# Quantised feed-forward in three stages cut another way: gate matmuls by themselves, the sigmoid in one stage with the second matmuls, 16-bit integers for the quantised values

## What is computed

```
x    = act_qdq(layernorm(h))             # scale = max|x| over the WHOLE batch / 32767, then round(x / scale) * scale
up   = act_qdq(x @ q(w_up).T)
gate = act_qdq(x @ q(w_gate).T)
sig  = clip(round(sigmoid(gate) * 65536), 0, 65535) / 65536
gate = act_qdq(gate * sig)
o    = act_qdq(gate * up)
h    = h + o @ q(w_down).T
```

## Time and profile before

| what | value |
|---|---|
| median of 3 runs | 5746.14 us |
| profiled execution, span from first to last instruction | 5746.7 us (no time of its own is recorded beside the span) |
| mean granted TensorE clock, share of full | 0.851 |
| `phase_b`, first matmul to last | 617.8 to 1058 us |
| `phase_c`, first ScalarE instruction to last of VectorE | 1071.6 to 1286.9 us |
| `phase_d`, first load issued to last of VectorE | 1291.6 to 1499.1 us |
| rest of the kernel | 0 to 617 us, and 1500 us to the end |

### The profile page before, as it was taken

How to read it: one execution, slowest core, us unless ns; L and a number is a source line. 1 busy time by engine, 2 the same in 40 slices (tenths; PEclk the granted TensorE clock), 3 DMA queues, 4 the chain that set the end, 5 groups by cost and what they waited for, 6 DMA issues and landing times. The chain is left out here.

```text
span 5746.7 us, 99792 instructions
## 1 busy us (share of the span) xinstructions
PE 4422.5 (77%) x26575; PEld 2884.0 (50%) x26575; DVE 3816.5 (66%) x9299; ACT 2478.7 (43%) x5698; POOL 596.5 (10%) x928
## 2 busy tenths in 40 slices
PE   6999788300388885878787776776999998689898
PEld 5777566200255553555555555554555554344444
DVE  4555333588687877777767764555777777477776
ACT  2222333565333333677777762222666666200000
POOL 0111000000000001000000001111111111122221
PEclk9999899655699997777777787887999999899998
DMA  2222233679644443222222225555333333211110
GB/s 81 74 75 68 105 140 139 196 240 396 229 132 124 132 124 91 62 71 71 71 71 71 71 52 144 156 156 139 85 91 92 92 90 88 63 46 47 49 47 25
DMA packets 380380, 617.00 MB, mean 107 GB/s; under 512 B 43575, under 2 KB 310389, under 8 KB 380277
## 3 DMA queue, kind: packets, MB, share of 16 engines
q1 hardware_dynamic: 367956, 614.35, 36.6%
q0 software_dynamic: 12320, 1.40, 0.2%
HBM read 345.02 MB, written 269.21 MB: 107 GB/s over the span
## 5 line engine op out<-in xcount | busy, mean ns | idle before, releaser
L1670 DVE TENSOR_REDUCE e_neg<-ps 91x1 f32<-91x273 f32 x1536 | 571.8, 427 | 139.2 <-PE ps L1491 131.8
L1603 ACT ACTIVATE e_probT<-ps 91x273 f32<-91x273 f32 x1536 | 491.6, 392 | 291.7 <-PE ps L1491 290.9
L1218 PE MATMUL ps<-k_downT,f_o 128*91 128x256 f32 x1152 | 259.7, 385 | 455.9 <-DVE f_o L1126 455.7
L2345 PE MATMUL ps<-m_we,m_xT 128*128 128x512 f32 x1104 | 530.8, 630 | 0.0
L1218 PEld LDWEIGHTS ps<-k_downT,f_o 128*91 128x91 f32 x1152 | 182.8, 161 | 524.5 <-issue 456.9
L1489 PE MATMUL ps<-c_mask_kq,c_identb 91*91 91x91 bf16 x1536 | 322.7, 241 | 105.9 <-ACT g_probT L1603 74.3
L1491 PE MATMUL ps<-e_k,e_q 96*91 96x273 bf16 x1536 | 344.3, 306 | 62.9 <-DMA e_k<-s_parts 28.1
L2279 DVE SCALAR_TENSOR_TENSOR m_acc<-ps,m_weight,m_acc 128x256 f32<-128x256 f32 x552 | 261.7, 481 | 185.7 <-PE ps L2345 175.9
L1491 PE MATMUL ps<-g_q,g_k 102*91 102x273 bf16 (+5 forms) x1536 | 328.5, 294 | 50.6 <-DVEq L1676 49.9
L2345 PEld LDWEIGHTS ps<-m_we,m_xT 128*128 128x128 f32 x1104 | 214.8, 202 | 227.9 <-issue 213.5
L1491 PE MATMUL ps<-e_q,e_k 128*91 128x273 bf16 x1536 | 285.7, 290 | 40.1 <-DMA e_q<-e_shift 38.2
(11 more groups left out here) (306 smaller groups left out, 9733.9 us busy)
## 6 DMA issues: line engine op xcount, KB each, us to landing
s_gate<-b_gu SPq DMA_DIRECT2D x32, 819.0 KB, 4.7
s_up<-b_gu SPq DMA_DIRECT2D x32, 819.0 KB, 6.1
c_g<-s_gate SPq DMA_DIRECT2D x32, 819.0 KB, 7.2
s_gated<-c_g SPq DMA_DIRECT2D x32, 819.0 KB, 8.6
d_g<-s_gated SPq DMA_DIRECT2D x32, 819.0 KB, 10.4
d_u<-s_up SPq DMA_DIRECT2D x32, 819.0 KB, 10.7
s_o<-d_o SPq DMA_DIRECT2D x32, 819.0 KB
f_o<-s_o SPq DMA_DIRECT2D x32, 819.0 KB, 4.8
```

What stands on the lines that cost most here:

```text
L1218: last = nc.tensor.matmul(ps[0:R, t // 2, (t % 2) * D:(t % 2 + 1) * D], o[:, u, k, t * R:(t + 1) * R], downT[:, k, :], start=(k == 0), sto ...
L1603: nc.scalar.activation(probT[0:R, p % 8, b, :], src, ACT.Exp, scale=float(HD) ** 0.5 if kinds[h] == COS else 1.0)\
L1670: last = nc.vector.tensor_reduce(neg[:, u, t, h:h + 1], src, AX.X, ALU.max, negate=True)
L2345: last = nc.tensor.matmul(ps[0:R, EBANK[m % 4], :], xT[:, u, k, t * R:(t + 1) * R], we[:, k, 2 * p:2 * p + 2, :].rearrange("p e d -> p (e ...
```

## The change

`phase_b` becomes `gate_stage`: only the gate matmuls; the rounded x is also stored to DRAM (`xq`). `up_stage` loads `xq` and gate, does the up matmuls, and beside them the rounding of gate, the sigmoid, the product and the maxima of gated and of up. `product_stage` takes the place of `phase_d`. All three are ordered by `pipeline`. PSUM is evacuated two banks at a time (128x546). ScalarE now writes x/scale directly into a 16-bit integer tile (the conversion rounds), so the separate VectorE rounding of gate, gated and up is gone, and the scales are folded into the scalar of one `scalar_tensor_tensor`.

```diff
+def multiply_pairs(nc, pe, ps, w, x, S, n):
+    for m in range(FP):                                   # FP = 3
+        pe.wait_ge(S["out"].sem, S["out"].at(back(n, 1), m + 1))   # back(n, 1): the image before
+        for f in (2 * m, 2 * m + 1):
+            for k in range(CT):
+                last = nc.tensor.matmul(ps[:, f, 0:T], w[:, k, f * 128:(f + 1) * 128], x[:, k, :], ...)
+        last.then_inc(S["mm"].sem, 1)
 # gate_stage, SyncE
+            def store_xq(n, u, i):
+                sp.wait_ge(S["xq"].sem, S["xq"].at(n))
+                sp.dma_start(xq_dram[batch_of(n)], x[:, u] ...)
+            def next_x(n, u, i):
+                    sp.wait_ge(S["mm"].sem, S["mm"].at(n))
+                    sp.wait_ge(xq_stored[u], 16 * (i + 1))
+                    load((n[0], n[1] + 2), u)
+            def store_gate(n, u, i):
+                sp.wait_ge(S["out"].sem, S["out"].at(n))
+            pipeline(sp, NB, ((store_xq, 1), (next_x, 0), (store_gate, 0)))
 # gate_stage, ScalarE, VectorE, TensorE
-                    for m in range(2 * FT):
-                        act.wait_ge(S["mm"].sem, S["mm"].at(n, m + 1))
-                        nc.scalar.copy(gu[:, u, m // FT, m % FT, :], ps[:, 4 * u + m % 4, 0:T])
+                for m in range(FP):
+                    act.wait_ge(S["mm"].sem, S["mm"].at(n, m + 1))
+                    nc.scalar.copy(gate[:, u, 2 * m:2 * m + 2, :], ps[:, 2 * m:2 * m + 2, 0:T])
+            pipeline(act, NB, ((divide, 1), (copy_gate, 0)))
+            pipeline(dve, NB, ((quantise, 1), (maximum, 0)))
+            pipeline(pe, NB, ((multiply, 0),))
 # up_stage
+        steps = sb("steps", [128, 2, N], mybir.dt.int16)
+        sig_steps = sb("sig_steps", [128, 2, N], mybir.dt.uint16)
+            pipeline(sp, NB, ((next_g, 1), (next_x, 0), (store_up, 0), (store_gated, 0)))
-                nc.scalar.activation(gm[:, u], g[:, u], ACT.Identity, scale=inv, bias=magic)
+                nc.scalar.activation(steps[:, u], g[:, u], ACT.Identity, scale=inv)
-                nc.scalar.activation(sg[:, u], gq[:, u], ACT.Sigmoid)
-                nc.scalar.activation(sm[:, u], sg[:, u], ACT.Identity, scale=65536.0, bias=magic)
+                nc.scalar.activation(sig[:, u], steps[:, u], ACT.Sigmoid, scale=scale)
+            pipeline(act, NB, ((divide, 1), (copy_up(0, 1), 0), (sigmoid, 1), (copy_up(1, FP), 0)))
-                nc.vector.tensor_scalar(gq[:, u], gm[:, u], MAGIC, scale, ALU.subtract, ALU.mult)
-                nc.vector.tensor_scalar(sm[:, u], sm[:, u], MAGIC + 65535.0, MAGIC, ALU.min, ALU.subtract)
+                nc.vector.tensor_scalar(sig_steps[:, u], sig[:, u], 65536.0, 65535.0, ALU.mult, ALU.min)
-                nc.vector.scalar_tensor_tensor(out=g2[:, u], in0=sm[:, u], scalar=1.0 / 65536.0,
-                                               in1=gq[:, u], op0=ALU.mult, op1=ALU.mult)
+                nc.vector.scalar_tensor_tensor(out=gated[:, u], in0=sig_steps[:, u], scalar=fine[:],
+                                               in1=steps[:, u], op0=ALU.mult, op1=ALU.mult)
+            pipeline(dve, NB, ((round_sigmoid, 0), (maximum_gated, -1), (product, 0), (maximum_up, -1)))
+            def multiply(n, u, i):
+                pe.wait_ge(x_loaded[u], 16 * (i + 1))
+                multiply_pairs(nc, pe, ps, upT, x[:, u], S, n)
 # product_stage
+            pipeline(sp, NB, ((following_loads, 1), (store, 0)))
-                        nc.scalar.activation(rounded[k][:, u], src[k][:, u], ACT.Identity, scale=inv[k],
-                                             bias=magic)
+                    nc.scalar.activation(steps[k][:, u], src[k][:, u], ACT.Identity, scale=inv[k])  # int16
-                        nc.vector.tensor_scalar(quant[k][:, u], rounded[k][:, u], MAGIC, scale[k], ...)
-                    nc.vector.tensor_tensor(o[:, u], quant["g"][:, u], quant["u"][:, u], ALU.mult)
+                nc.vector.scalar_tensor_tensor(out=o[:, u], in0=steps["g"][:, u], scalar=both[:],
+                                               in1=steps["u"][:, u], op0=ALU.mult, op1=ALU.mult)
+            pipeline(dve, NB, ((product, 0), (maximum, -1)))
```

More of the change, by code:

```diff
@@ L637, in _, with divide @@
                 S[k].give(act)
[L638 to L648, removed]
[L649 to L652 removed]
+            def divide(n, u, i):
+                act.wait_ge(x_loaded[u], 16 * (i + 1))
+                act.wait_ge(S["xq"].sem, S["xq"].at(back(n, 2)))
+                nc.scalar.activation(xm[:, u], x[:, u], ACT.Identity, scale=inv, bias=magic)\
+                    .then_inc(S["xm"].sem, 1)
@@ L654, in _, with copy_gate @@
+            def copy_gate(n, u, i):
+                act.wait_ge(stored[u], 16 * i)
+                act.wait_ge(S["max"].sem, S["max"].at(back(n, 2)))
+                for m in range(FP):
+                    act.wait_ge(S["mm"].sem, S["mm"].at(n, m + 1))
+                    nc.scalar.copy(gate[:, u, 2 * m:2 * m + 2, :], ps[:, 2 * m:2 * m + 2, 0:T])\
+                        .then_inc(S["out"].sem, 1)
+            pipeline(act, NB, ((divide, 1), (copy_gate, 0)))
         @block.vector
         def _(dve):
-            for k in ("xq", "newg", "maxg", "newu", "maxu"):
+            for k in ("xq", "new", "max"):
@@ new lines, in _, with divide, sigmoid, copy_up @@
+        @block.scalar
+        def _(act):
+            for k in ("steps", "sig", "out"):
+                S[k].give(act)
+            def divide(n, u, i):
+                act.wait_ge(g_loaded[u], 16 * (i + 1))
+                act.wait_ge(S["gated"].sem, S["gated"].at(back(n, 2)))
+                nc.scalar.activation(steps[:, u], g[:, u], ACT.Identity, scale=inv).then_inc(S["steps"].sem, 1)
+            def sigmoid(n, u, i):
+                act.wait_ge(S["steps"].sem, S["steps"].at(n))
+                act.wait_ge(S["sig_steps"].sem, S["sig_steps"].at(back(n, 2)))
+                nc.scalar.activation(sig[:, u], steps[:, u], ACT.Sigmoid, scale=scale).then_inc(S["sig"].sem, 1)
+            def copy_up(first, end):
+                def stage(n, u, i):
+                    if first == 0:
+                        act.wait_ge(up_stored[u], 16 * i)
+                        act.wait_ge(S["maxu"].sem, S["maxu"].at(back(n, 2)))
+                    for m in range(first, end):
+                        act.wait_ge(S["mm"].sem, S["mm"].at(n, m + 1))
+                        nc.scalar.copy(up[:, u, 2 * m:2 * m + 2, :], ps[:, 2 * m:2 * m + 2, 0:T])\
+                            .then_inc(S["out"].sem, 1)
+                return stage
+            pipeline(act, NB, ((divide, 1), (copy_up(0, 1), 0), (sigmoid, 1), (copy_up(1, FP), 0)))
@@ L753, in _ @@
-            pipeline(act, NB, ((sigmoid, 1), (divide, 2)))
+                act.wait_ge(S["o"].sem, S["o"].at(back(n, 2)))
+                for k in "gu":
+                    act.wait_ge(loaded[k][u], 16 * (i + 1))
+                    nc.scalar.activation(steps[k][:, u], src[k][:, u], ACT.Identity, scale=inv[k])\
+                        .then_inc(S[k].sem, 1)
+            pipeline(act, NB, ((divide, 1),))
         @block.vector
         def _(dve):
-            for k in ("gq", "sr", "g2", "new", "max"):
+            for k in ("o", "new", "max"):
```

327 lines of the change are left out of this document (151 added, 176 removed).

## The result

| | kernel before | changed kernel |
|---|---|---|
| median (4 runs each) | 5747.8 us (5734.66 to 5758.03) | 5510.0 us (5507.18 to 5534.94) |
| profiled span | 5746.7 us | 5506.1 us |

The account below looks back on a forecast made before the run. It took TensorE to bound the first stage, VectorE the second and the DMAs the third: 5746.7 - 257.8 + 26.5 - 6 = 5509.4, so 5509 us, range 5480 to 5570.

Parts of the forecast that it names:

- step 1: First stage without the up matmuls: 5.7 us an image, 182.4 us in place of 440.2, -257.8 us.
- x rival: First stage bound by x, its load chain longer than its cover: 6.8 us an image, 5545 us in all; chance 0.07.
- Second stage, VectorE: Second stage set by VectorE: a turn of 7.01 us, 7.4 an image with waits; stage 241.8 us, +26.5.
- Second stage, the others: Second stage's ScalarE 5.1, TensorE 5.5 and DMAs 7.0 us an image, all under VectorE's 7.4.
- The tightest place: Second stage's DMAs: 2.80 MB an image at 400 GB/s, 7.0 us, as long as VectorE's turn.
- DMA rival: DMAs bind the second stage at 306 GB/s: 9.1 us an image, +82 us, 5565 us in all; chance 0.14.
- Third stage: Third stage's body stays DMA-bound at 6.3 us an image; only its end shortens, -6 us (0 to -14).
- Around: Outside the three stages: one `set_scale` moves behind the second stage, its 1.2 us paid either way; no change.
- the clock: Rival: short pauses hold TensorE at 1.2 GHz; both stages 5795 us (chance 0.01), second alone 5625 (0.02).

Follow-up runs that it names:

- first experiment: Changed kernel with the first stage's load of the next x issued ahead of the store of rounded x: first stage 179.4 us instead of 192.7, median 5508.34 us.
- late load of x: Changed kernel with the second stage's load of the next x issued behind both stores: second stage 248.6 us against 230.0, 5532.15 us in all.
- no maximum: Changed kernel without the maximum of up in the second stage: second stage 233.3 us against 230.0.
- old third stage: Changed kernel with the third stage of the kernel before (`phase_d`, float roundings): third stage 211.2 us instead of 202.9, span 5509.7 us.
- float32 tiles: Changed kernel with the second stage's two 16-bit tiles made float32, same instructions: second stage 233.5 us against 230.0, span 5511.0 us.

## Why the prediction was right, and where only its total was

1. *First stage.* -247.5 instead of -257.8. What failed is the chain in step 1. I reckoned two images long, from the end of n's matmuls to n+2, "5.1 us, against the 5.5 that image n+1 gives as cover", and counted the store ahead of the load only for the bandwidth it takes. It costs by its wait: the store waits for the rounding of the very x whose load was issued a turn before, so every load waits for the load ahead of it, and two buffers work as one. That chain can be summed from rows of before: landing 3.1, 0.84 and 0.51, three issues and semaphores. It is 6.0 here. The first experiment shows it: with the order turned, my 5.5 to 5.7 came out at once, 179.4 us over 32 images. The order listing in the section on the change has the store and its wait ahead of the load; I had asked what that store moves, and not what it waits for. The x rival (6.8) had x as what TensorE waits for, with the wrong mechanism. What I held against it was also misread: 245 of 400 GB/s leaves the DMA engines free for under 40% of the time, not "over half", and their share was 0.65.

2. *Second stage, VectorE.* +14.7 instead of +26.5. The mechanism was right and the turn mis-sized: 7.04 us and not 7.4. The allowance of 0.26 an image for the turn of the loop was the "issue" idle of before (5.9 + 2.5 us), and 0.13 was added for stores. With a turn of work ahead, all "issue" idle is 3.1 us and the wait for stores 3.4 us in the stage, 0.2 an image together. The turn itself came out shorter than the 7.01 summed from before, too: where nothing is waited for, it is 6.73 us from one rounding to the next. The 16-bit rounding at 1.0 us was right, and the product at 1.87 was 0.06 short for a reason that the narrow type has no part in.

3. *Second stage, the others.* "The tightest place" was right: removing VectorE's work alone gained nothing. The DMA rival at 306 GB/s fell, 387 was held over the whole stage. That 400 would be held was more luck than knowledge: variants of this stage moved 364 to 397 GB/s at a share of 1.00 to 1.02. The Trainium skill's 358 GB/s ("DMA: Bandwidth & Descriptors", Specifications) would give 7.8 us an image; the trace shows 7.04 at 387, and 413 in the third stage, so here the measurement decides against it. The Trainium skill's other rule ("Vector Engine (DVE) Microarchitecture Reference", 5.1 Performance modes), one-source operations at two results a cycle whatever the width, agrees: 1012 ns with 16-bit, 1011 with 32-bit output. TensorE hid, and the clock stayed up in the loop, with its longest pause at 1.68 us, where 1.86 brought a fall in another kernel.

4. *Third stage.* -4.6 instead of -6, again by a near cancellation. I had left the body at 6.3 us an image and put the gain at the end, with "one product and one maximum" after ScalarE. The end grew by 1.6 us, since the last products wait for stores, and since each product goes ahead of the maximum of the image before, so that one product alone is never left with one maximum. The -6 was also reckoned by unequal marks: the 10.2 us of before run from the start of ScalarE's last instruction (1488.7), the 4.0 from its end. By its end the old tail is 8.6, and my own reasoning gives -4.6; that this is what was measured is luck. The body shrank by 6.4, since the rate rose to 413 GB/s, which I had only at the edge of the range. That the stage is bound by its DMAs was right: VectorE is busy 61% of the body where it was 91%.

5. *Around.* 1.8 us less in front of the second stage, where one `set_scale` left. I had cost it at nothing both ways; behind the stage nothing was added (4.5 instead of 4.7).

The rivals: the clock did not fall in the loops of the changed kernel. Made to pause longer, in the late load of x, the second stage kept a clock of 0.96 and lost 19 us and not 142, and none of the 19 can be found at the falls. A clock that stays at half over a whole stage was not brought about in any run.

## What to carry to other kernels

A queue that issues loads and stores in order couples what the buffers keep apart: for every DMA ahead of a load, ask what it waits for, and follow that wait back until it meets the load itself. Put loads that only need a free buffer ahead of stores that need fresh data. Where two engines or an engine and the DMAs tie, take both away at once as well, since one alone shows next to nothing. Do not take a busy share near 1, of TensorE or of the DMAs, for a bound: look at what ends the waits. And sum a prediction by stages, so that a total that agrees can still be seen to rest on errors that cancel.

## What the runs showed of the hardware

- One VectorE instruction over 128x1638 takes some 60 ns more with a factor read from a tile than with a constant: 1925 and 1866 (two sources), 1075 and 1011 (one source). On ScalarE it was 1573 with neither, 1661 to 1664 with scale or bias from a tile, 1760 with both.
- 16-bit input or output changed no VectorE or ScalarE duration here, in either direction.
- In the loops of the second stages (changed kernel, first experiment, no maximum, old third stage, float32 tiles, late x) TensorE's clock fell after some pauses of 1.86 to 2.56 us, 13 of 29, and not after others of the same length (2.06, 2.23, 2.33, 2.51); it fell after none of the shorter ones, up to 1.85 us. Beside another bound a fall cost no time: in the late load of x an image with one took 7.4 to 7.8 us from start to start.
- The same three 819 KB transfers an image moved at 391, 400 and 413 GB/s, each over 186 us or more with the engines' share at 1.01, beside 89, 91 and 61% of VectorE.
- The four transfers an image of the second stage moved at 397, 395, 392, 389, 381 and 364 GB/s from 830 to 1030 us, all with the share between 1.00 and 1.02 (changed kernel, old third stage, float32 tiles, first experiment, no maximum, late x), and the share was 0.97 at 345 GB/s where TensorE set the pace.
